# A graph-network kernel: GpSimd waits for every twelfth of its gathers and scatters to land

## The chip, the cores and the metric

The kernel runs on one core of one Trainium2 chip. The metric is the device time of one execution in microseconds (us). The time before is 6714.79 us, the median of 3 runs (6712.42 to 6715.54).

## The reference, cut to what matters

Four blocks of graph layers run one after another over 6250 nodes with 128 features and 106250 edges sorted by target. Each block is added to its input and normalised over the features.

```python
def _sage_conv(h, src, dst, Wl, bl, Wr):          # block 0, twice: stages 0 and 1
    agg = segment_sum(h[src], dst) / maximum(deg, 1.0)[:, None]
    return agg @ Wl.T + bl + h @ Wr.T
def gcn_conv(x, edge_index, W, b):                # block 1 once, block 2 twice: stages 2, 3, 4
    h = x @ W
    return segment_sum(h[src] * (dinv[src] * dinv[dst])[:, None], dst) + b
for l in range(3):                                # block 3: nine "hops", stages 5 to 13
    out = h @ W[l, 0]; x = h
    for k in (1, 2, 3):
        x = segment_sum(w[:, None] * x[src], dst)  # w = dinv[src] * edge_weight * dinv[dst]
        out = out + x @ W[l, k]
    h = relu(layernorm(h + out + bias[l]) * gamma[l] + beta[l])
x = layernorm(x + block(x))
```

So there are 14 sums over neighbours, which the kernel calls stages, and each needs all rows of the one before.

## The kernel before, in words

The nodes make 49 tiles of 128 (`TILES`). In each stage TensorE forms the sum over neighbours in two ways at once, as a `Split` lays down.

**Dense tiles.** For most target tiles the kernel has a matrix in HBM: `counts` (bf16, how many edges join two nodes) for stages 0 to 4, `weights` (float32) for stages 5 to 13. SyncE loads it into `room` in units, and TensorE multiplies every source tile with it (`sweep`, L1130 for bf16 in three parts, L1134 for float32). A stage of 0 to 4 (`EARLY` and its kin) has 41 dense tiles in 11 groups, nine of them four tiles wide. A hop stage (`LATE`) has 31 dense tiles in 8 groups, seven four tiles wide and one three wide; each group takes 49 blocks, one for each source tile.

**Sparse tiles.** The other 8 (in a hop stage 18) target tiles are summed from their edges. GpSimd gathers 128 source rows at a time from `table` in HBM into one of 36 slots of `ring_f` (`fast`, L690: one indirect DMA of 64 KB). A pair of tiles takes 36 gathers, so a stage of 0 to 4 has 144 and a hop stage has 324. VectorE builds a one-hot matrix for each (L1707), and TensorE multiplies them (`edges`, L1164) in batches of three gathers, of which a hop stage has 108. TensorE's program is one fixed order: the sweep is cut into beats of some three blocks, and each batch of `edges` stands behind a beat (`beat_of`). A batch waits for its gathers by `chunk_in[slot]`, and everything behind it on TensorE waits as well.

**What paces GpSimd.** Ahead of a gather it waits for the slot to be free (`batch_done`), and for every second gather for the sweep to have come far enough (`unit_used`, by `pace`). At a stage's start it waits until all rows of the last stage are written (`rows_out`); the stage's other work has begun by then.

**Who writes the matrices.** GpSimd scatters ones and edge weights into zeroed HBM, 128 elements in one indirect DMA (`scatter`, L646). `counts` takes three lists of 215, 285 and 225 scatters, all before GpSimd's first gather. 90 of them come first, then 21 gathers of tables (L662), then the rest. `weights` takes 532, which are issued between the gathers of stages 1 to 4, 161, 80, 150 and 141 of them (`QUOTA`). A scatter already waits for those 4 or 5 places back in its list (6 or 7 for `weights`), by `scattered[q]`, since two writes to one place must not meet.

**The start.** Before stage 0, VectorE prepares the lists and TensorE walks over all edges to sum the degrees (`degree_walk`, L981 and L1528, 49 iterations of 42 matmul records). GpSimd scatters meanwhile. Stage 0's sweep follows the walk; its first sparse batch stands at beat 108 of 182.

Of the kernel before, what the change touches and what calls it, by code (L numbers as in the profile page):

```python
# [139 lines left out]
def landed_by(which, q):  # L140
    return sum(p.lap for p in LISTS[:which] if q < p.laps)
# [4 lines left out]
PAIR0 = [sum(p.pairs for p in SPLITS[:a]) for a in range(STG + 1)]  # L146
# [15 lines left out]
WB = SPAN // HB  # L162
assert SPAN % HB == 0 and HOTS * WIN <= (SPAN - 7) * P and SPAN >= MIX + 3 and SPAN >= BODY
AHEAD_UNITS = 6


def pace(a, c):
# [36 lines left out]
def program(nc, A, out):  # L204
    ctx = ExitStack()
    with ctx:
# [6 lines left out]
        def sem(name):  # L213
            return ctx.enter_context(nc.semaphore(name))
# [174 lines left out]
        scattered = [sem(f"scattered{q}") for q in range(QS)]  # L389
        v_begun, off_ready, fast_rows, p_fast, v_x, in_h, fast_go, parts_rdy = names(  # L390
            "v_begun off_ready fast_rows p_fast v_x in_h fast_go parts_rdy")
        chunk_in = [sem(f"chunk_in{c}") for c in range(CHP)]
# [228 lines left out]
        @block.gpsimd  # L621
        def _(pool):
            pool.iota(iota_i[:, :], pattern=[[1, P]], base=0, channel_multiplier=0).then_inc(g_const, 1)
            pool.iota(ci[:, :], pattern=[[P, CG]], base=0, channel_multiplier=1).then_inc(g_const, 1)
            pool.iota(step_i, pattern=[[1, STEPS]], base=0, channel_multiplier=0).then_inc(g_const, 1)
            pool.memset(ones[:, :], 1.0).then_inc(g_const, 1)
            pool.memset(ident[:, :], 0.0).then_inc(g_const, 1)
            pool.wait_ge(g_const, 5)
            pool.affine_select(out=ident[:, :], in_=ident[:, :], compare_op=ALU.not_equal, fill=1.0, base=0,
                               pattern=[[-1, P]], channel_multiplier=1).then_inc(g_const, 1)  # L630

            for c in range(CHP):
                pool.memset(lows[:, :, c:c + 1], float(LOWS[c])).then_inc(g_lows, 1)

            def scatter(which, i):
                p, m = LISTS[which], (weights if which == NC else counts).rearrange("s (n a) -> (s n) a", a=1)
                r, q = divmod(i, p.laps)

                beside = (q + 1) % p.laps
                if r or which:  # L640
                    if landed_by(which, q) + r:
                        pool.wait_ge(scattered[q], (landed_by(which, q) + r) * 16)
                    if landed_by(which, beside) + r + (q == p.laps - 1):
                        pool.wait_ge(scattered[beside], (landed_by(which, beside) + r + (q == p.laps - 1)) * 16)
                at = q * p.lap + r
                pool.indirect_dma_start(  # L646
                    out=m, out_offset=bass.IndirectOffsetOnAxis(ap=lane_idx[which][:, at:at + 1], axis=0),
                    in_=lane_val[which][:, at:at + 1], in_offset=None).then_inc(scattered[q], 16)

            pool.wait_ge(lanes_ready, 1)  # L650
            wait_zeroed(pool, zeroed_counts, ZQ, 4 * CUTS[1])
            for i in range(AHEAD_OF_ROWS):
                scatter(0, i)

            pool.wait_ge(off_ready, 1)
            pool.wait_ge(e_out, 96)
            blocks = [(k, rows_d.bitcast(I32), e_dst) for k in range(RBLOCKS)]
            blocks += [(k, rows_w, e_wgt) for k in range(RBLOCKS)] + [(k, rows_s.bitcast(I32), e_src) for k in range(WBLOCKS)]
            for k, rows_, pad in blocks:
                n = min(RB * CHP, (PAIRS - 1 - k * RB) * CHP + MIX + 3)  # L660
                runs = pad.rearrange("(e a) -> e a", a=1)
                pool.indirect_dma_start(out=rows_[0:n, k, :], out_offset=None, in_=runs[:, :],  # L662
                                        in_offset=bass.IndirectOffsetOnAxis(ap=off_i[0:n, k:k + 1], axis=0)
                                        ).then_inc(window_rows if pad is e_dst and k < WBLOCKS else fast_rows, 16)

            def fast():
                for i in range(AHEAD_OF_ROWS, LISTS[0].lane):
                    scatter(0, i)
                for which in range(1, NC):
                    pool.wait_ge(lanes_ready, which + 1)  # L670
                    wait_zeroed(pool, zeroed_counts, ZQ, 4 * CUTS[which + 1])
                    for i in range(LISTS[which].lane):
                        scatter(which, i)
                pool.wait_ge(lanes_ready, NC + 1)
                assert sum(QUOTA) == LISTS[NC].lane
                for a, p in enumerate(SPLITS):
                    rows_from = A["x"] if a == 0 else tables[a % 2]
                    if a:
                        pool.wait_ge(rows_out, GROUP0[a] * 16)
                    if a == 1:  # L680
                        wait_zeroed(pool, zeroed_weights, 1, LATE.zeros)
                    put = 0
                    for c in range(p.pairs * CHP):
                        pair, slot = divmod(c, CHP)
                        if PAIR0[a] + pair > 0:
                            freed = (PAIR0[a] + pair - 1) * STP + slot
                            pool.wait_ge(batch_done, freed // HB + 1)
                        if a and c % 2 == 0 and pace(a, c) > 0:
                            pool.wait_ge(unit_used, UNIT0[a] + pace(a, c))
                        pool.indirect_dma_start(out=ring_f[:, slot, :], out_offset=None, in_=rows_from[:, :],  # L690
                                                in_offset=bass.IndirectOffsetOnAxis(ap=f_src[:, c:c + 1], axis=0)
                                                ).then_inc(chunk_in[slot], 16)
                        while 0 < a < STAGES and put * p.pairs * CHP < (c + 1) * (QUOTA[a] - WINDOW):
                            scatter(NC, sum(QUOTA[:a]) + put)
                            put += 1
                    while 0 < a < STAGES and put < QUOTA[a]:
                        scatter(NC, sum(QUOTA[:a]) + put)
                        put += 1

            def whole(way):  # L700
                for q in range(LISTS[0].laps):
                    pool.wait_ge(scattered[q], len(range(q, AHEAD_OF_ROWS, LISTS[0].laps)) * 16)
                pool.wait_ge(pad_out, 48)
                pool.wait_ge(v_walk, 1)
                for k in range(CG):
                    for rows_, pad in ((dstep, dst_pad), (wstep, wgt_pad)):
                        pool.indirect_dma_start(out=rows_[:, k, :], out_offset=None, in_=pad[:, :],
                                                in_offset=bass.IndirectOffsetOnAxis(ap=chunk_idx[:, k:k + 1], axis=0)
                                                ).then_inc(walk_dma, 16)
                stages(pool, way, gather)  # L710

            def gather(way, a, kind, layer):
                if kind == 0:
                    pool.wait_ge(v_tabs, 1)
                    pool.wait_ge(x_copied, 16)
                else:
                    pool.wait_ge(table_done, a * (GROUPS * 16))
                    pool.sem_inc(pool_go, 1)

                def lap(it, n):  # L720
                    for s in range(0, n, SUB):

                        pool.wait_ge(pe_step, way.step(a) + it * RING + (s + SUB - NQ))
                        if s % NQ == 0:
                            pool.wait_ge(idx_staged, a * (way.chunks // NQ) + it * (RING // NQ) + (s // NQ + 1))
                        pool.sem_inc(pool_go, 1)
                        for c in range(s, s + SUB):
                            pool.indirect_dma_start(out=ring[:, c, :], out_offset=None, in_=table[:, :],
                                                    in_offset=bass.IndirectOffsetOnAxis(ap=stage[:, c:c + 1], axis=0)
                                                    ).then_inc(landed[c % NQ], 16)  # L730
                laps, rest = divmod(way.chunks, RING)
                with pool.Fori(0, laps) as it:
                    lap(it, RING)
                if rest:
                    lap(laps, rest)
            ways(pool, "pool", fast, whole)
# [1285 lines left out]
```

## Time and profile before

| | |
|---|---|
| time, median of 3 runs | 6714.79 us |
| span of the profiled execution, first to last instruction | 8546.7 us |
| mean granted TensorE clock in it | 0.929 |
| TensorE busy (PE) | 6464.8 us, 76% |
| GpSimd busy (POOL) | 4719.2 us, 55% |
| VectorE busy (DVE) | 2178.6 us, 25% |

The profiled execution has no time of its own beside its span. Its span is 1831.9 us (27%) longer than the median of the runs, so a duration from the trace has to be weighed before it is set into a run's time. On the page the second part cuts the span into 40 equal slices; each digit is the busy share in tenths, 9 standing for 90% or more.

### The profile page before, as it was taken

Reading aid. Unit: us, or ns where it says so; the run is one execution under the profiler, and the core shown is the slowest. Engines: PE = TensorE matmul, PEld = TensorE weight load, DVE = VectorE, ACT = ScalarE, POOL = GpSimd, SP = SyncE. Lnnn points to the kernel's source line nnn. Section 1 sums busy time; section 2 is a strip of 40 time slices with the busy share of each in tenths; the row PEclk is TensorE's granted clock in tenths of the full one; section 3 lists DMA queues with packets and bytes.
Section 4 is the critical chain, followed back from the end, with each engine's and each line's share of the span. In section 5 each row is a group of like instructions: output and inputs, shape, how many; then the busy total and the mean of one; then the engine's idle time right before and its main releaser. Section 6 shows DMA issues by size and latency. Waiting matters only on the chain.

```text
span 8546.7 us, 79040 instructions
## 1 busy us (share of the span) xinstructions
PE 6464.8 (76%) x27152; PEld 3836.3 (45%) x27153; DVE 2178.6 (25%) x8464; ACT 316.1 (4%) x856; POOL 4719.2 (55%) x4960
## 2 busy tenths in 40 slices
PE   0003039998878787896998988888888898989888
PEld 0003039655544444443554544455444454554444
DVE  8235014222222211121221223222121231212144
ACT  0000000000000000000000000000000000000000
POOL 3766740034545466464656656565565656656565
PEclk9999999999988888997998999999999999999999
DMA  9047000365546554564676767666667676667776
GB/s 369 5 187 299 0 11 0 122 190 153 166 126 205 167 169 146 182 193 170 248 242 233 253 243 251 241 245 232 240 250 241 249 256 230 243 238 253 254 251 220
DMA packets 605834, 1703.64 MB, mean 199 GB/s; under 512 B 132490, under 2 KB 351043, under 8 KB 503944
## 3 DMA queue, kind: packets, MB, share of 16 engines
q1 hardware_dynamic: 340474, 1337.92, 44.4%
q0 software_dynamic: 157616, 240.14, 9.6%
q10 hardware_dynamic: 107388, 120.98, 4.0%
q8 instruction: 205, 3.36, 0.2%
q14 instruction: 151, 1.24, 0.0%
HBM read 1476.47 MB, written 223.40 MB: 199 GB/s over the span
## 4 chain that ended last, share of the span: by engine, by line
PE 64%; another core or an unknown queue 17%; issue 13%; DVE 3%; SPq 1%; ACT 1%; DMA 0%; DVEq 0%; POOL 0%; ACTq 0%; POOLq 0%
PE pwide L1134 32%; PE pwide L1130 15%; PE pstep L1164 8%; PE pstep L981 5%; PE pwide L1222 1%; SPq L537 0%; DVE ring_f L1329 0%; PE pwide L1180 0%; PE pwide L1221 0%; DVE lane_val L1335 0%; DVE lane_val L1336 0%; SPq L517 0%; DVE ring_f L1332 0%; PE pwide L1184 0%
## 5 line engine op out<-in xcount | busy, mean ns | idle before, releaser
L690 POOL DMA_INDIRECT ring_f<-table,f_src x3492 | 3319.3, 951 | 2553.9 <-issue 933.9
L1134 PE MATMUL pwide<-room,acc 128*128 128x512 f32 (+1 forms) x3920 | 1856.4, 612 | 88.6 <-issue 83.3
L1134 PE MATMUL pwide<-room,hcur 128*128 128x512 f32 (+1 forms) x3136 | 1486.8, 611 | 69.5 <-issue 68.1
L1164 PEld LDWEIGHTS pstep<-hot,ring_f 128*128 128x128 f32 x7272 | 1047.7, 199 | 739.0 <-issue 670.2
L1164 PE MATMUL pstep<-hot,ring_f 128*128 128x64 f32 x7272 | 1014.7, 272 | 315.1 <-issue 296.6
L1707 DVE TENSOR_SCALAR hot<-iota,f_win,f_wgt 128x64 f32<-128x64 f32 x2916 | 720.5, 328 | 2053.1 <-PE pstep L1164 856.5
L981 PE MATMUL pstep<-acc,hot 128*128 x2058 | 445.4, 350 | 850.7 <-DVE deg_sums L1533 611.8
L1134 PEld LDWEIGHTS pwide<-room,acc 128*128 128x128 f32 x3920 | 735.0, 199 | 786.1 <-issue 740.0
L1130 PE MATMUL pwide<-room 128*128 128x512 bf16 (+2 forms) x2695 | 1012.7, 377 | 52.0 <-issue 51.2
L646 POOL DMA_INDIRECT counts<-lane_val,lane_idx x725 | 712.7, 983 | 399.5 <-issue 243.8
L1130 PE MATMUL pwide<-room,hcur 128*128 128x512 bf16 (+2 forms) x2695 | 829.6, 374 | 59.2 <-issue 50.4
L1134 PEld LDWEIGHTS pwide<-room,hcur 128*128 128x128 f32 x3136 | 585.5, 198 | 632.7 <-issue 594.0
L981 PEld LDWEIGHTS pstep<-acc,hot 128*128 128x128 f32 x2058 | 444.5, 332 | 851.6 <-issue 851.6
L1130 PE MATMUL pwide<-room,acc 128*128 128x512 bf16 (+2 forms) x2156 | 638.7, 379 | 39.2 <-issue 38.8
L646 POOL DMA_INDIRECT weights<-lane_val,lane_idx x532 | 521.5, 980 | 163.2 <-issue 159.2
L690 POOL DMA_INDIRECT ring_f<-in_x,f_src x144 | 140.6, 976 | 673.0 <-PE pstep L1164 618.5
L1130 PEld LDWEIGHTS pwide<-room 128*128 128x128 bf16 x2695 | 269.6, 100 | 358.6 <-issue 108.1
L1130 PEld LDWEIGHTS pwide<-room,hcur 128*128 128x128 bf16 x2695 | 272.3, 103 | 327.4 <-issue 96.0
L1730 DVE SCALAR_TENSOR_TENSOR xres<-pwide,dinv,xres 128x128 f32<-128x128 f32 x294 | 83.4, 344 | 1015.9 <-remote 546.6
L1130 PEld LDWEIGHTS pwide<-room,acc 128*128 128x128 bf16 x2156 | 217.2, 103 | 257.4 <-issue 81.5
L1730 DVE SCALAR_TENSOR_TENSOR zz<-pwide,dinv,xres 128x128 f32<-128x128 f32 x196 | 55.5, 344 | 741.4 <-remote 421.0
L1528 DVE TENSOR_SCALAR hot<-iota,f_dst 128x128 f32<-128x128 f32 x1029 | 209.6, 285 | 108.0 <-remote 57.9
(318 smaller groups left out, 2486.7 us busy)
## 6 DMA issues: line engine op xcount, KB each, us to landing
room<-weights SPq DMA_DIRECT2D x693, 1024.0 KB
room<-counts SPq DMA_DIRECT2D x495, 512.0 KB
room<-weights SPq DMA_DIRECT2D x162, 768.0 KB
weights<-zz SPq DMA_DIRECT2D x56, 1792.0 KB
counts<-zz ACTq DMA_DIRECT2D x44, 1568.0 KB
ring_f<-table,f_src POOLq DMA_INDIRECT x3492
room<-counts SPq DMA_DIRECT2D x100, 384.0 KB
room<-weights SPq DMA_DIRECT2D x63, 512.0 KB
```

The costliest lines, as they stand in the source:

```text
L646: pool.indirect_dma_start(out=m, out_offset=bass.IndirectOffsetOnAxis(ap=lane_idx[which][:, at:at + 1], axis=0), in_=lane_val[which][:, at ...
L690: pool.indirect_dma_start(out=ring_f[:, slot, :], out_offset=None, in_=rows_from[:, :], in_offset=bass.IndirectOffsetOnAxis(ap=f_src[:, c: ...
L981: ins = pe.matmul(pstep[0][:, 0:2], hot[:, j, :], degree_of[:, bass.ds(it * SPAN + j, 1), :].rearrange("p c a -> p (c a)"), start=j == 0, ...
L1130: ins = pe.matmul(bank[:, 0:w * P], part[:, first + o, :], room_short[:, n % SLOTS, o * w * P:(o + 1) * w * P], start=begins and i == 0, s ...
L1134: ins = pe.matmul(bank[:, 0:w * P], x_of(a)[:, first + o, :], room[:, n % SLOTS, o * w * P:(o + 1) * w * P], start=begins, stop=ends)
L1164: ins = pe.matmul(bank[:, low:low + WIN], row, one, start=begins, stop=ends and not own, skip_group_check=True)
L1222: ins = pe.matmul(o, z, w3[:, of + k, :], start=True, stop=True)
L1528: ins = V.tensor_scalar(hot[:, j, :], iota[:, :], f_dst_flat[:, bass.ds(it * SPAN + j, 1)], None, ALU.is_equal)
L1707: return V.tensor_scalar(to, iota[:, 0:WIN], at, f_wgt[:, pair * CHP + c:pair * CHP + c + 1], ALU.is_equal, ALU.mult)
L1730: ins = V.scalar_tensor_tensor(to[:, j, :], po[:, j, :], scale_of(kind)[:, first + j:first + j + 1], more(j), ALU.mult, ALU.add)
```

## The change

After every twelfth gather of a stage (counted from the stage's start) GpSimd waits until this gather has landed, before it does anything else. After every twelfth scatter of a list (counted from the list's start) it waits until this scatter is written. Nothing else is changed; no instruction moves.

```diff
+REST_AT = 12
@@ scatter(which, i)
                 pool.indirect_dma_start(
                     out=m, out_offset=bass.IndirectOffsetOnAxis(ap=lane_idx[which][:, at:at + 1], axis=0),
                     in_=lane_val[which][:, at:at + 1], in_offset=None).then_inc(scattered[q], 16)
+                if i % REST_AT == REST_AT - 1:
+                    pool.wait_ge(scattered[q], (landed_by(which, q) + r + 1) * 16)
@@ fast(), in the loop over the gathers c of stage a
                         pool.indirect_dma_start(out=ring_f[:, slot, :], out_offset=None, in_=rows_from[:, :],
                                                 in_offset=bass.IndirectOffsetOnAxis(ap=f_src[:, c:c + 1], axis=0)
                                                 ).then_inc(chunk_in[slot], 16)
+                        if c % REST_AT == REST_AT - 1:
+                            pool.wait_ge(chunk_in[slot], (PAIR0[a] + pair + 1) * 16)
                         while 0 < a < STAGES and put * p.pairs * CHP < (c + 1) * (QUOTA[a] - WINDOW):
                             scatter(NC, sum(QUOTA[:a]) + put)
```

## Rows read from the trace of the kernel before

**Rows 1.** The page's first and second part: busy time, and 40 slices.
```profile
PE 6464.8 (76%) x27152; PEld 3836.3 (45%) x27153; DVE 2178.6 (25%) x8464; ACT 316.1 (4%) x856; POOL 4719.2 (55%) x4960
...
PE   0003039998878787896998988888888898989888
...
POOL 3766740034545466464656656565565656656565
```

**Rows 2.** Windows over four hop stages: length, busy of each engine, clock, DMA share, GB/s.
```profile
4480.50:4982.20 501.70, 449.53 (x1582) 250.31 (x1581) 102.17 (x394) 21.49 (x62) 307.73 (x325) 0.92 0.70 248
4982.20:5490.10 507.90, 450.63 (x1549) 251.35 (x1548) 148.39 (x611) 25.83 (x75) 307.00 (x324) 0.92 0.71 249
6008.60:6519.00 510.40, 447.27 (x1582) 250.61 (x1581) 102.59 (x392) 21.49 (x62) 308.72 (x325) 0.92 0.70 244
7023.30:7540.20 516.90, 452.29 (x1702) 262.44 (x1701) 100.70 (x378) 27.50 (x75) 305.96 (x324) 0.92 0.68 235
```

**Rows 3.** Line L690 in 4982.2:5490.1: min/median/max ns; idle until, us, times.
```profile
L690 POOL DMA_INDIRECT ring_f<-table,f_src x324: 938/944/1141, 4982.2 to 5455.6; - x162
...
  issue: 86.4, 278
  PE pstep L1164: 32.1, 23
  DMA table<-acc: 27.6, 1
  PE pwide L1134: 25.6, 16
  remote: 23.3, 6
```

**Rows 4.** Timeline of POOL at a hop stage's start: gathers 1, 2, 3 and 12.
```profile
7023.26 0.94 POOL L690 DMA_INDIRECT ring_f<-table,f_src  x1 [32.99 <-DMA table<-acc]
7024.51 0.94 POOL L690 DMA_INDIRECT ring_f<-table,f_src  x1 [0.30 <-issue]
7025.76 0.94 POOL L690 DMA_INDIRECT ring_f<-table,f_src  x1 [0.30 <-PE pwide L1134]
...
7037.05 0.94 POOL L690 DMA_INDIRECT ring_f<-table,f_src  x1 [0.30 <-issue]
```

**Rows 5.** Timeline of PE there, where it waits for gathers to land.
```profile
7027.67 0.63 PE L1164 MATMUL pstep<-hot,ring_f 128*128 128x64 f32 x4 [1.97 <-DMA ring_f<-table,f_src]
7029.67 0.69 PE L1164 MATMUL pstep<-hot,ring_f 128*128 128x64 f32 x2 [1.37 <-DMA ring_f<-table,f_src]
...
7042.81 0.43 PE L1164 MATMUL pstep<-hot,ring_f 128*128 128x64 f32 x2 [0.91 <-DMA ring_f<-table,f_src]
```

**Rows 6.** Timeline of PE in a stretch of a hop stage without a stall.
```profile
5037.69 2.79 PE L1134 MATMUL pwide<-room,acc 128*128 128x512 f32 x6
5040.32 0.78 PE L1164 MATMUL pstep<-hot,ring_f 128*128 128x64 f32 x6
5040.94 1.94 PE L1134 MATMUL pwide<-room,acc 128*128 128x512 f32 x4
5042.71 1.05 PE L1222 MATMUL pwide<-w,zz 128*128 128x128 f32 x8
5043.60 0.78 PE L1164 MATMUL pstep<-hot,ring_f 128*128 128x64 f32 x6
```

**Rows 7.** The chain of work: the degree walk, and a sweep in bf16.
```profile
738.63 9.13 PE pstep L981 x42
748.31 9.13 PE pstep L981 x42
...
1627.08 30.43 PE pwide L1130 x141
```

**Rows 8.** Windows of the start (columns as in rows 2).
```profile
312.00:470.00 158.00, 0.00 (x0) 0.00 (x0) 39.38 (x108) 0.00 (x0) 120.02 (x124) 1.00 0.02 0
470.00:604.00 134.00, 0.00 (x0) 0.00 (x0) 44.32 (x84) 0.00 (x0) 89.79 (x87) 1.00 0.52 211
...
801.00:1220.00 419.00, 49.13 (x233) 51.74 (x233) 24.61 (x111) 0.00 (x0) 289.28 (x298) 1.00 0.11 38
```

**Rows 9.** Waits of POOL, whole run: in total us, times, longest.
```profile
POOL ring_f L690 <- PE pstep L1164: 960.7, 197, 604.7
```

**Rows 10.** Waits of POOL in stage 1 (2010.7:2566), same columns.
```profile
POOL ring_f L690 <- PE pwide L1130: 90.7, 19, 12.7
POOL ring_f L690 <- DMA table<-zz: 52.5, 1, 52.5
...
POOL weights L646 <- DMA weights<-lane_val,lane_idx: 0.6, 2, 0.3
```

**Rows 11.** Timeline of POOL: the first list's second scatter, and its sixth.
```profile
85.17 0.98 POOL L646 DMA_INDIRECT counts<-lane_val,lane_idx  x1 [0.31 <-issue]
...
92.26 0.97 POOL L646 DMA_INDIRECT counts<-lane_val,lane_idx  x1 [2.30 <-DMA counts<-lane_val,lane_idx]
```

## The prediction

> **What bounds the kernel now.** The page first [rows 1]: from the seventh slice on TensorE (PE) is busy eight or nine tenths, GpSimd (POOL) four to six. That names TensorE. But busy counts only the 0.94 us in which GpSimd works on a gather; what matters is from one start to the next. The windows over hop stages [rows 2] show a period of 502 to 517 us with some 450 us of TensorE and 307 of GpSimd. The waits of line L690 in one of them [rows 3] show the rest: 324 gathers at 944 ns, 86.4 us of "issue" (the 0.30 us between two starts, of which the timeline is full [rows 4]), 27.6 us at the start for the last stage's rows, and 32.1+25.6+23.3 = 81 us for slots and pace, of which some 14 us are again the 0.30 us of those 45 times. So GpSimd needs 324 x 1.25 = 405 us and 28 to 33 us of start: 433 to 438 us in a period of 508. Its true slack in the trace is about 70 us a hop stage, not the half that the digits suggest.
>
> **How the trace stands to the runs.** The span is 1832 us over the median of 6714.79, so the runs have less slack still. I rebuild the run from stretches without a stall. A hop stage on TensorE: three blocks of L1134 take 2.63 us (5037.69 to 5040.32), so 0.877 a block, 7 x 49 blocks make 301 us, and the three wide group's 49 at three quarters 32 us; a batch of L1164 takes 0.62 us (5040.32 to 5040.94), 108 make 67 us; the work behind 13 groups of tiles at 0.9 us for one, two or more such each, 27 us [rows 6]. Sum 427 us. A stage of 0 to 4: 141 records of L1130 in 30.43 us, 0.216 each [rows 7]; 9 x 49 x 3 make 286 us, the two narrow groups 40, the batches 30, the rest 35: about 390. The walk is 49 x 9.69 = 475 us [rows 7]. The start up to its end is 1582 us in the trace, but the stretch 801:1220 holds six iterations (58 us) in 419, and 312:604 holds 84 us of VectorE in 292 [rows 8]; without these stalls, and with 20 us kept for a load that VectorE awaits there, it is about 1030. Total 1030 + 5 x 390 + 9 x 427 + 30 for the end = 6853, 2% over the median. I read that as: in the runs TensorE is at full pace nearly throughout, and a hop stage takes about 420 us.
>
> Then GpSimd must keep up with 420. With 25 us for the stage's start (28 to 33 in the trace, scaled), a gather can take at most 395/324 = 1.22 us from start to start. The ends for this price p are 0.944 (its own duration alone) and 1.25 (as traced, which would make a hop stage 430 and the total too long). I take 1.17, near the traced end, since the duration is steady and only the 0.30 us beside it is what a run without a recorder could shorten. So GpSimd has 404 of 420 us: 16 us of slack.
>
> **What the change adds.** 60 waits in stages 0 to 4 (12 each), 243 in the hops (27 each), and for scatters 17+23+18 = 58 in the lists of counts and 13+7+12+12 = 44 in stages 1 to 4. Nothing is removed or moved. The instruction behind a wait is the next gather or scatter, and everything of GpSimd stands in that line. The price of one wait is the time from the end of GpSimd's instruction to the landing, L. The trace has it where TensorE waits for a gather [rows 4, 5]: the second ended at 7025.45, and its matmuls begin at 7027.67 (2.2 us); the third at 7026.70 and 7029.67 (3.0); the twelfth, the first that would be waited for, at 7037.99 and 7042.81 (4.8). Below, L could be near 2, above near 4.8. I take 2.5, since the first two have TensorE standing ready and the third may have had another cause for part of it.
>
> The Trainium skill, "DMA: Bandwidth & Descriptors", section "Anatomy of one DMA — SWDGE (gpsimd) path", gives a fixed 2.0 us for a DMA issued by GpSimd, most of it the receipt of the last write, plus bytes over 436 GB/s: 2.15 us for 64 KB. The trace's smallest, 2.2, agrees. By that page alone the hop term below would be 27 x 2.15 = 58 us a stage in place of 68.
>
> *Hop stages.* GpSimd before: 324 x 1.17 + 25 = 404, under TensorE's 420. After: 404 + 27 x 2.5 = 472. TensorE is fed in its fixed order and the ring is empty at a stage's start (gather 1 comes only when the sweep is under way, and TensorE already waits for it [rows 5]), so the 36 slots give no cushion against a slower feeder. The period goes from 420 to 472: +52, times 9 = **+468 us**.
>
> *Stages 1 to 4.* Slower start: 52.5 us in the trace [rows 10], 43 taken. Stage 1 has 144+161 = 305 issues: 357 + 43 = 400 (TensorE 390), after it 25 waits of 2 us more, 450: +50. Stage 2: 224 issues, 305 us, after it 343 under 390: 0, hidden by the sweep. Stage 3: 294, 387, then 24 waits: 435, +45. Stage 4: 285, 376, then 424: +34. Together **+129 us**. I take 2 us here since matrices of bf16 load HBM less, and a scatter is smaller. For a scatter's landing the trace has an upper row only: the second ended at 86.15 and the sixth, which waits for it, starts at 92.26 after its usual 0.30, so 5.8 us, while HBM is being zeroed [rows 11]; later the waits 6 or 7 places back cost nothing [rows 10]. The lower bound is 0.
>
> *Start and stage 0.* 58 waits at 0.8 to 2 us delay GpSimd by 45 to 115 us. Cover: it then stands 604.7 us until TensorE's first batch in the trace [rows 9]. In a run the walk ends near 1030 and the first sparse batch comes 108/182 of a stage later, near 1240; GpSimd has its scatters done near 1040 and the first 36 gathers near 1085, so about 150 us cover it. The third list is needed at the eighth group, near 1240 too. Price 0; with the cover gone, up to +100. Stage 0's 108 gathers behind the first ring have 80 beats, 1.5 us each or more: enough.
>
> Sum: 6714.79 + 468 + 129 = 7312, say **7310 us**.
>
> **The rivals.**
> - *Forecast, 0.58:* GpSimd becomes the bound in the hops, by 30 to 65 us a stage: 7080 to 7450.
> - *GpSimd is already at its traced pace in the runs, or L is nearer 3 (0.17).* Then no slack hides anything: 27 x 2.7 = 73 a hop stage, 657, and 50+48+46 early, and 20 of the start: 7535. For it speaks that 0.30 stands unchanged in all rows of POOL; against it the total of 6853, already too long without it.
> - *GpSimd is quicker than 1.1 from start to start (0.19).* With 1.05 it takes 340 + 25, plus 68 is 433 against 420: +13 x 9, early +20, so 6850; with 1.0 nothing shows. In the trace itself the 81 us of waits for slots nearly cover 68 us. For it speaks that slack, against it that a run has 90 us a stage less than the trace, which can only come off this slack.
> - *The wait is met when it is reached (0.02):* a landing within the 0.30 us between starts; no change. [Rows 5] exclude it for gathers.
> - *Other side, faster (0.04):* while GpSimd issues without a pause, TensorE and VectorE stand: 801:1220 loses 361 us [rows 8]. If that is in the runs too, a pause of 1 to 2 us in every 15 gives back a tenth, 35 us at the start, and some 10 us of stall a hop stage; it decides if GpSimd has 70 us of slack in a run as in the trace: 6640. The sum of 6853 speaks against such stalls in the runs. The Trainium skill, "SBUF — State Buffer", section "Who interferes with whom", has an exclusive lock between VectorE and GpSimd that could be such a stall; no row shows it as one.
>
> **How the numbers follow.** A measurement tells 0.2% (13 us) from nothing. Slower by more: 0.58 + 0.17 + 0.14 of the third = 0.89; within: the third's other 0.05 and the 0.02 of a wait that is met = 0.07; faster: 0.04. The range reaches from the quick rival's 6850, leaving out what of it and of the fast one lies below (near 0.14), to the second's 7535 above, leaving out an L of 3 and more: 6850 to 7540.
>
> **What the profile after should show.** 303 waits of L690 for ring_f's own DMA, idle 2.8 us on average with the 0.30; GpSimd's waits for slots and pace in a hop stage down from 81 to under 40 us; TensorE waiting for ring_f in every hop stage, not in a few; hop periods of 510 to 550 in the trace, the span 8700 to 9050, for there the slack is larger than in the runs. The start: stage 0's sweep begins where it did. Wrong would be the price p if the time rises under 200 us with the waits at 2.5 us each; wrong L if the waits are under 1.5 us; wrong the reading of the runs if trace and runs rise alike.

## The result, and the profile after

| | before | after |
|---|---|---|
| time, median of 3 runs | 6714.79 us | 7676.65 us (7647.36 to 7689.74) |
| ratio | | 1.1425 (95%: 1.1391 to 1.1458) |
| span of the profiled execution | 8546.7 us | 7645.5 us |

The change costs 962 us. The forecast was 7310 and its range ended at 7540, so it is 367 us short and outside its range. The span of the trace after is the time of a run; that of before was not. The execution behind [rows 1 to 11] was unlike every other one that was recorded in this study, which matters for all that follows.

The page after, first and second part (answers to [rows 1]):

```profile
span 7645.5 us, 79062 instructions
...
PE 6364.7 (83%) x27152; PEld 3789.7 (50%) x27153; DVE 2182.1 (29%) x8464; ACT 316.6 (4%) x856; POOL 4715.5 (62%) x4960
...
PE   0039996999889989789989888998898899988887
...
POOL 2666766666666666666665665656666656566565
PEclk9755598999999999999999999999999999999999
```

The windows over four hop stages after, with the columns of [rows 2]:

```profile
3632.90:4136.90 504.00, 447.79 (x1582) 249.97 (x1581) 103.78 (x393) 21.54 (x62) 307.46 (x325) 0.96 0.74 247
4136.90:4639.80 502.90, 450.26 (x1549) 248.04 (x1548) 148.42 (x609) 25.85 (x75) 306.72 (x324) 0.95 0.75 252
4639.80:5137.90 498.10, 449.50 (x1707) 258.96 (x1706) 102.37 (x381) 27.55 (x75) 305.90 (x324) 0.96 0.73 244
5137.90:5640.30 502.40, 444.69 (x1582) 247.79 (x1581) 103.98 (x393) 21.54 (x62) 308.34 (x325) 0.96 0.74 248
```

A period of 502 us looks like that of [rows 2]. The periods of before that it has to be held against are about 428 us; they come below, from a second profile of the kernel before.

The gather's line in the third of these windows (answers to [rows 3]): idle until, us, times, and from issue to landing.

```profile
  issue: 104.0, 264
  DMA ring_f<-table,f_src: 81.7, 24
  PE pwide L1139: 7.3, 14
  PE pstep L1169: 6.7, 22
...
DMA to landing us min/median/max: 2.5/3.8/6.2
```

24 of the 27 waits bear the name of the gather's own landing, 81.7/24 = 3.40 us each with the usual 0.30. The waits for slots and pace are down to 14 us, 36 times, of which 11 us are again the 0.30: TensorE hardly ever holds GpSimd up. The timeline of GpSimd around two of the waits:

```profile
4707.06 0.94 POOL L693 DMA_INDIRECT ring_f<-table,f_src  x1 [0.30 <-issue]
4708.31 0.99 POOL L693 DMA_INDIRECT ring_f<-table,f_src  x1 [0.30 <-issue]
4712.61 0.94 POOL L693 DMA_INDIRECT ring_f<-table,f_src  x1 [3.32 <-DMA ring_f<-table,f_src]
...
4726.34 0.94 POOL L693 DMA_INDIRECT ring_f<-table,f_src  x1 [0.30 <-issue]
4730.70 0.94 POOL L693 DMA_INDIRECT ring_f<-table,f_src  x1 [3.42 <-DMA ring_f<-table,f_src]
```

One gather, 1.25 us from start to start, and once in twelve 4.3 us. TensorE in the same 33 us:

```profile
4702.47 0.69 PE L1169 MATMUL pstep<-hot,ring_f 128*128 128x64 f32 x2 [3.66 <-DMA ring_f<-table,f_src]
...
4719.12 0.43 PE L1169 MATMUL pstep<-hot,ring_f 128*128 128x64 f32 x2 [0.21 <-DMA ring_f<-table,f_src]
...
4723.02 0.43 PE L1169 MATMUL pstep<-hot,ring_f 128*128 128x64 f32 x2 [0.44 <-DMA ring_f<-table,f_src]
```

It stands three times for a gather that has only now landed: it takes each one as it comes. Over the whole run it waits like this for 608 us (first row; the second is stage 0, where it stands 61.3 us for the first gather), and GpSimd's waits for landings are these:

```profile
PE pstep L1169 <- DMA ring_f<-table,f_src: 608.1, 450, 15.8
...
PE pstep L1169 <- DMA ring_f<-in_x,f_src: 75.5, 20, 61.3
```

```profile
POOL ring_f L693 <- DMA ring_f<-table,f_src: 762.5, 234, 6.0
POOL counts L647 <- DMA counts<-lane_val,lane_idx: 233.5, 141, 6.6
...
POOL ring_f L693 <- DMA weights<-lane_val,lane_idx: 81.1, 29, 3.9
...
POOL weights L647 <- DMA ring_f<-table,f_src: 67.1, 23, 4.5
```

### The profile page after: what moved, and what is told of

Its sections match the earlier page's. It is cut to its first block and busy times, and to the rows that moved or that the text cites. A ratio compares the mean times of both kernels' runs of the same rounds, so it can differ in the third digit from the quotient of the medians.

```text
span 7645.5 us, 79062 instructions
## 1 busy us (share of the span) xinstructions
PE 6364.7 (83%) x27152; PEld 3789.7 (50%) x27153; DVE 2182.1 (29%) x8464; ACT 316.6 (4%) x856; POOL 4715.5 (62%) x4960
## 5 line engine op out<-in xcount | busy, mean ns | idle before, releaser
L1139 PE MATMUL pwide<-room,acc 128*128 128x512 f32 (+1 forms) x3920 | 1827.3, 608 | 37.3 <-DMA room<-weights 37.3
L1169 PE MATMUL pstep<-hot,ring_f 128*128 128x64 f32 x7272 | 1073.2, 274 | 688.8 <-DMA ring_f<-table,f_src 608.1
L1139 PE MATMUL pwide<-room,hcur 128*128 128x512 f32 (+1 forms) x3136 | 1470.7, 611 | 0.0
L647 POOL DMA_INDIRECT counts<-lane_val,lane_idx x725 | 716.6, 988 | 501.5 <-DMA counts<-lane_val,lane_idx 233.5
L1135 PE MATMUL pwide<-room 128*128 128x512 bf16 (+2 forms) x2695 | 995.8, 370 | 0.0
L1135 PE MATMUL pwide<-room,acc 128*128 128x512 bf16 (+2 forms) x2156 | 615.6, 370 | 0.5 <-ACT zz L788 0.5
L788 ACT ACTIVATE zz<-pwide 128x512 f32<-128x512 f32 (+2 forms) x127 | 73.3, 577 | 4350.3 <-PE pwide L1139 2855.5
L1711 DVE TENSOR_SCALAR hot<-iota,f_win 128x64 f32<-128x64 f32 x720 | 131.7, 272 | 278.6 <-PE pstep L1169 276.4
```

The lines of the kernel that those rows point to most:

```text
L647: pool.indirect_dma_start(out=m, out_offset=bass.IndirectOffsetOnAxis(ap=lane_idx[which][:, at:at + 1], axis=0), in_=lane_val[which][:, at ...
L788: act.activation(zT, bank[:, 0:w * P], ACT.Copy).then_inc(z_done, 1)
L1135: ins = pe.matmul(bank[:, 0:w * P], part[:, first + o, :], room_short[:, n % SLOTS, o * w * P:(o + 1) * w * P], start=begins and i == 0, s ...
L1139: ins = pe.matmul(bank[:, 0:w * P], x_of(a)[:, first + o, :], room[:, n % SLOTS, o * w * P:(o + 1) * w * P], start=begins, stop=ends)
L1169: ins = pe.matmul(bank[:, low:low + WIN], row, one, start=begins, stop=ends and not own, skip_group_check=True)
L1711: return V.tensor_scalar(to, iota[:, 0:WIN], at, None, ALU.is_equal)
```

## The experiments

The theories: **A**, GpSimd issues at 1.25 us in the runs as in the trace and bounds the whole run, so each pause is paid, wherever it stands; **B**, the forecast's account (slack of 16 us in a hop stage, stage 2 and the start covered).

**1. The waits of the lists of counts alone (58), ahead of stage 0.**

```diff
-                if i % REST_AT == REST_AT - 1:
+                if which < NC and i % REST_AT == REST_AT - 1:
```

The gathers' waits are taken out.

> Only the 58 waits in the three lists of counts (17+23+18), none on gathers or weights. Theory A (GpSimd is the bound of the whole run, from its first scatter on, at 1.25 us from start to start as traced): each wait is paid in full, 58 x 1.8 = +105 us on 6715. Theory B (the forecast: GpSimd has some 150 us of cover at the start, TensorE bounds there): no change, 0 to +15 us.

Measured: 6799.06 us, ratio 1.0116 (1.0099 to 1.0133), +80. B's cover of 150 us isn't there, only a small one: in this run's trace stage 0's first gather starts at 1253.07, 107 us later than in the second profile of before (1145.71, experiment 8), and of these GpSimd gets 22 us back in its wait ahead of stage 1, which is 22.6 us in place of 44.4.

**2. The waits of the hop stages alone (243).**

```diff
-                        if c % REST_AT == REST_AT - 1:
+                        if a >= STAGES and c % REST_AT == REST_AT - 1:
```

The scatters' waits are taken out.

> Only the 243 waits on gathers of the nine hop stages. Theory A: 243 x 2.35 = +571 us, since GpSimd has no slack. Theory B, with 16 us of slack a stage and L 2.5: +468 us; with L 2.35: +427 us.

Measured: 7383.7 us, 1.0995 (1.0976 to 1.1015), +664: 73.8 a stage, 2.73 for each wait. That is over both expectations, and nearest to the rival's 657.

**3. The waits of stages 0 to 4 alone (60 of gathers, 44 of scatters).**

```diff
-                if i % REST_AT == REST_AT - 1:
+                if which == NC and i % REST_AT == REST_AT - 1:
@@
-                        if c % REST_AT == REST_AT - 1:
+                        if a < STAGES and c % REST_AT == REST_AT - 1:
```

> Only the 60 waits on gathers of stages 0 to 4 and the 44 on scatters of weights. Theory A: 104 x 2.1 = +218 us, stage 0 and stage 2 included, and with e1 and e2 it adds up to the 962 us of the whole change. Theory B: +129 us, nothing from stages 0 and 2.

Measured: 6919.56 us, 1.0298 (1.0281 to 1.0315), +200. The three parts make 944 of the 962 us: the cost lies in all of them and adds up.

**4. Half as many waits.**

```diff
-REST_AT = 12
+REST_AT = 24
```

> All waits, but every twenty-fourth instead of every twelfth: some 200 waits. Theory A (no slack, each wait paid): half of 962, +480 us. Theory B (the slack is used up first): a hop stage 404 + 14 x 2.4 = 438 against 420, +18 x 9, and +60 early: +220 us. In the profile: if the trace of before is long because GpSimd never pauses, this one's span should lie between, above its own run's time.

Measured: 7199.54 us, 1.0712 (1.0694 to 1.073), +480, half of 962 (481). With slack, the first waits would have been free and half of them would have cost less than half. The span was 7204.5 us, the time of its runs. This also ended an idea that I held for a while, that the long trace of before came from a GpSimd that never pauses.

**5. All 303 waits of gathers, each on the gather six places back.**

```diff
-                            pool.wait_ge(chunk_in[slot], (PAIR0[a] + pair + 1) * 16)
+                            pool.wait_ge(chunk_in[slot - 6], (PAIR0[a] + pair + 1) * 16)
```

The scatters' waits are taken out.

> Every twelfth gather's place waits for the gather six places back, which by the trace landed within 4.8 us and was issued 6 x 1.25 us earlier: a wait instruction that is met when it is reached; no waits on scatters. If the price of the change is the time to the landing: no change on 6715. If a wait as such breaks up GpSimd's stream (a restart cost of its own), +303 times that cost, 30 us for 0.1.

Measured: 6718.04 us, 1.0006 (0.9996 to 1.0015). Over the 303 waits the interval runs from −3 to +10 us, so a wait instruction that is met when it is reached costs 0.03 us at most; what costs is the landing.

**6. The kernel before with less work for TensorE.**

```diff
+                elif o == 1 and not begins and not ends and o != nb - 1:
+                    return
```

> The kernel before, in which TensorE leaves out the second block of each unit of weights that is at least three tiles deep in the hop stages: 12 of 49 blocks in each group, about 82 us of TensorE a stage; loads, waits and GpSimd's work are unchanged. The output is not the reference's. Theory A (GpSimd is the bound): 6715 less at most some 5 us a stage at the hand-over, so 0 to -50 us. Theory B (420 of TensorE over 404 of GpSimd): -16 a stage, -144 us. TensorE alone as the bound: -700 us.

Measured: 6674.28 us, 0.9943 (0.9927 to 0.996), −38 us. The blocks left out are some 80 us a hop stage at the pace of [rows 6]; TensorE's busy time falls by less, by about 50 us: each of the remaining records of the sweep takes longer (615 ns in the mean in place of 589), at a mean granted clock of 0.95 where it was 0.99 to 1.00. One hop stage of this trace (columns of [rows 2]), which in the second profile of before takes 429.70 us with 424.55 of TensorE:

```profile
4118.10:4539.80 421.70, 375.03 (x1518) 224.23 (x1517) 103.32 (x382) 27.54 (x75) 306.57 (x324) 0.95 0.83 289
```

TensorE then waits for ring_f instead. Its waits in that trace, and in the next experiment's:

```profile
PE pstep L1166 <- DMA ring_f<-table,f_src: 476.2, 482, 5.9
```

```profile
PE pstep L1166 <- DMA ring_f<-table,f_src: 25.7, 18, 5.8
```

**7. The kernel before with every twelfth gather of the hops not issued (243 of 2916).**

```diff
+                        if a < STAGES or c % 12 != 11:
+                            (the indirect DMA of fast(), as before)
@@
+                if a < STAGES or i % 12 != 11:
+                    (the wait of TensorE for it, as before)
```

> The kernel before, in which every twelfth gather of the hop stages is not issued and TensorE does not wait for it (it multiplies what the slot held): 27 of 324 gathers a stage, 34 us of GpSimd. The output is not the reference's. Theory A: -34 x 9 = -304 us, or less where TensorE becomes the bound at its own 400 to 420 us a stage. Theory B: 0, TensorE bounds already.

Measured: 6651.09 us, 0.9909 (0.9892 to 0.9925), −62 us: 7 of the 34 us a stage that GpSimd has less. Now GpSimd waits for TensorE. Its waits from 4300 to 6600 us in this trace come to 0.60 us each in the first row, where the 331 of the whole second profile of before (experiment 8) are 0.33 us each; and a hop stage in which TensorE never stands:

```profile
POOL ring_f L691 <- PE pstep L1166: 114.8, 192, 6.2
POOL ring_f L691 <- PE pwide L1135: 60.6, 111, 4.9
```

```profile
4554.71:4970.06 415.35, 415.35 (x1582) 237.30 (x1581) 105.04 (x392) 21.49 (x62) 282.52 (x297) 1.00 0.87 295
```

Experiments 6 and 7 together place the bound: taking work from TensorE gives 4 us a stage, from GpSimd 7, and then the other one holds. Against a period of about 428 us, GpSimd alone would need about 424 and TensorE alone about 421. So the two are close in the kernel before, but whatever is added to GpSimd's line makes it the later one nearly at once.

**8. The kernel before, unchanged, profiled again.**

> The kernel before once more, for a second trace of it. Its time: 6715 us, no change. Open is the span: if the recorder itself stretches a kernel whose GpSimd never pauses, about 8500 us again; if the first trace caught one odd execution, 6720 us, with the stalls of TensorE and VectorE in the start gone, hop stages of about 430 us, and GpSimd in them with no idle time beside the 0.30 us between gathers.

Measured: 6721.51 us, 1.0002 (0.9993 to 1.0012), and its span is the time of a run. First the page, and the windows over four hop stages and the start:

```profile
span 6713.0 us, 79040 instructions
...
PE 6076.4 (91%) x27152; PEld 3685.3 (55%) x27153; DVE 2184.9 (33%) x8464; ACT 316.2 (5%) x856; POOL 4725.7 (70%) x4960
```

```profile
3715.70:4146.40 430.70, 422.46 (x1554) 237.83 (x1553) 149.35 (x611) 25.84 (x75) 306.65 (x324) 1.00 0.86 296
4146.40:4576.10 429.70, 424.55 (x1702) 250.12 (x1701) 101.35 (x378) 27.49 (x75) 306.01 (x324) 0.99 0.83 282
4576.10:4999.00 422.90, 417.61 (x1582) 238.17 (x1581) 104.66 (x393) 21.48 (x62) 308.14 (x324) 1.00 0.87 294
...
801.00:1220.00 419.00, 401.97 (x1959) 276.39 (x1960) 112.16 (x476) 8.64 (x15) 311.63 (x323) 1.00 0.45 131
```

The gather's line in the second of these windows, and GpSimd's timeline at two places: the hand-over from the lists of counts to stage 0, and from stage 2 to stage 3.

```profile
L690 POOL DMA_INDIRECT ring_f<-table,f_src x324: 940/944/1016, 4146.4 to 4549.9; - x162
...
  issue: 83.8, 275
  DMA table<-hcur: 25.6, 1
  PE pstep L1164: 10.1, 33
  PE pwide L1134: 4.6, 15
```

```profile
1144.35 1.05 POOL L646 DMA_INDIRECT counts<-lane_val,lane_idx  x1 [0.31 <-issue]
1145.71 1.17 POOL L690 DMA_INDIRECT ring_f<-in_x,f_src  x1 [0.30 <-issue]
...
2081.31 0.96 POOL L646 DMA_INDIRECT weights<-lane_val,lane_idx  x1 [0.31 <-issue]
2082.57 0.97 POOL L690 DMA_INDIRECT ring_f<-table,f_src  x1 [0.30 <-issue]
```

This is the profile that the prediction should have had. The 81 us of waits for slots and pace [rows 3] are 14.7 us, 48 times the 0.30. All 324 gathers stand 1.25 us apart, 404 us from the first start to the last, and the rest of the period is the hand-over of the rows. TensorE is 98 to 99% busy in a hop stage and GpSimd 71 to 73%, and yet GpSimd is the later of the two. The two hand-overs show it in the early part: the last scatter of counts is followed by stage 0's first gather after 0.30 us, and stage 2's last scatter likewise by stage 3's first gather. The window 801:1220 has TensorE busy for 402 us where [rows 8] have 49.

**9. The 243 waits of the hops, on the gather before the last.**

```diff
-                            pool.wait_ge(chunk_in[slot], (PAIR0[a] + pair + 1) * 16)
+                            pool.wait_ge(chunk_in[slot - 1], (PAIR0[a] + pair + 1) * 16)
```

Otherwise as experiment 2.

> As e2 (243 waits in the hop stages), but each waits for the gather before the last instead of the last, which was issued 1.25 us earlier. If a wait costs the time to a landing: 2.73 - 1.25 = 1.5 us each, +360 us in place of the 664 of e2. If it costs a fixed sum for emptying or restarting GpSimd's DMA queue: +664 us again.

Measured: 7132.15 us, 1.0612 (1.0594 to 1.063), +413, 1.70 us for each. A landing of 3.0 us less one spacing of 1.25 leaves 1.75; a fixed price of a wait that blocks would have stayed at 2.73. Held against experiment 2, the wait has become 1.03 us cheaper, a little less than one spacing.

**10. The same 243 places, but GpSimd works for 2 us there in place of waiting.**

```diff
-                            pool.wait_ge(chunk_in[slot], (PAIR0[a] + pair + 1) * 16)
+                            for n in range(2):
+                                rests[0] += 1
+                                pool.memset(f_dst_flat, 0.0).then_inc(g_const, 1)
+                                pool.wait_ge(g_const, 6 + rests[0])
```

> As e2, but in place of the landing GpSimd writes zeros twice to a table of 128 x 1029 that is no longer read, some 2.2 to 2.6 us in each of the 243 places. Theory A (any time of GpSimd is paid in full): 243 x 2.4 = +580 us. If it is the empty DMA queue that costs, and not GpSimd's time: nothing near that, below +200 us. Theory B of the forecast, 16 us of slack a stage: +440 us.

Measured: 7145.47 us, 1.063 (1.0612 to 1.0648), +426, 1.75 us for each. The memsets were shorter than I had assumed. GpSimd's timeline:

```profile
5006.33 0.95 POOL L694 DMA_INDIRECT ring_f<-table,f_src  x1 [0.31 <-issue]
5007.28 1.99 POOL L700 MEMSET f_dst<- 128x1029 f32 x2
5009.53 0.95 POOL L694 DMA_INDIRECT ring_f<-table,f_src  x1 [0.27 <-POOL f_dst L700]
```

From the end of a gather to the next one's start it is 2.25 us, 1.95 more than the usual 0.30. Of the 243 pauses 8 fall into a hand-over between two hop stages, in which GpSimd waits anyway (a stage's last gather is its 324th, a twelfth one), and one stands behind the very last gather. The other 234 make 456 us. The eight hand-overs, from the end of a stage's last gather to the start of the next one's first, are shorter than in the second profile of before, 156 us together against 187. 456 − 31 = 425, and 426 was measured. The same sum for experiment 2, with hand-overs of 158 us: (664 + 29)/234 = 2.96 us for a landing. So each microsecond of pause inside a stage is paid, less some 4 us a stage that the hand-over gives back, and what counts is GpSimd's time, not the drained queue of its transfers.

**11. The waits of stage 2 alone (19).**

```diff
-                if i % REST_AT == REST_AT - 1:
+                if which == NC and sum(QUOTA[:2]) <= i < sum(QUOTA[:3]) and i % REST_AT == REST_AT - 1:
@@
-                        if c % REST_AT == REST_AT - 1:
+                        if a == 2 and c % REST_AT == REST_AT - 1:
```

> Only stage 2's waits: 12 on its gathers and 7 on its scatters. Theory A (GpSimd bounds in stage 2 too, whose sweep has two bf16 parts instead of three): 19 x 1.9 = +36 us. The forecast's step (stage 2 has 390 us of TensorE over 305 of GpSimd, so its waits are hidden): 0.

Measured: 6749.57 us, 1.0051 (1.0037 to 1.0064), +35. The stage for which the forecast had 0, "hidden by the sweep", pays like the others: 1.86 us for each wait, against 1.93 for the 104 of experiment 3.

**12. A version that might be faster: the hops' sparse batches are spread over one beat less, so that the last one stands a beat earlier.**

```diff
-LATE = Split([4, 4, 4, 4, 2], [4] * 7 + [3], 9, -2, last=2)
+LATE = Split([4, 4, 4, 4, 2], [4] * 7 + [3], 9, -1, last=2)
```

> A try at a faster kernel: the kernel before with the hop stages' sparse batches spread over one beat less (the last one stands one beat, 3.2 us of TensorE, earlier), no waits added. If the hand-over after the last gather has TensorE's beat on its path: up to -3 us a stage, -25 us. If the last gather's landing, 3 us, is the later of the two: 0. If batches that come earlier only wait more: 0 to +10 us.

Measured: 6730.8 us, 1.0026 (1.0016 to 1.0037), +17. No version that does all the work is faster than the kernel before (those of experiments 6 and 7 leave some out).

## Why the prediction was wrong, point by point

**Right: what the change does.** The instruction behind a wait is the next gather, all of GpSimd's line stands behind it, the ring gives no cushion, and GpSimd sets the time. The 303 waits came as written, and so did TensorE waiting for ring_f in every hop (48.4 us in the window above, 5.1 in one of the second profile of before). The waits for slots and pace stand at 14 us, as forecast under 40, but that is no merit: they were 14.7 before the change. The hop periods, forecast at 510 to 550, are 498 to 504 in the four windows above. TensorE's 427 us of a hop stage, rebuilt from rows without a stall, is near: experiment 7 puts its floor at about 421.

**Wrong: the price p = 1.17, and with it 16 us of slack.** It is 1.25 us in every trace, 404 us for 324 gathers, and the hand-over takes the rest of the 428. In a hop stage there is no slack but some 4 us in the hand-over; +52 was to be +74. Of these 22 us, 16 are the slack; the rest is the next point, less what falls into the hand-over. Over nine stages it is 664 in place of 468, 196 us.

**Why p went wrong: the sum of 6853.** It was 2% over the median and I used it to rule out p = 1.25. The misfit lay elsewhere. The records of the sweep (L1130) in stages 2 and 3 of the second profile of before, and in stage 2 of the first one: length, PE busy (records), clock, DMA share, GB/s.

```profile
1756.50:2065.30 308.80, 236.95 (x1078) 0.97 0.80 251
2065.40:2443.40 378.00, 336.92 (x1617) 1.00 0.73 211
```

```profile
2544.90:2964.90 420.00, 252.75 (x1078) 0.86 0.58 185
```

A stage of 0 to 4 has 539 blocks (11 groups of 49). Stage 2 has two records for each, as `parts_of` in the kernel says, and the sum had three: it put down 390 us for a sweep that takes 309. The first trace had this count too. And stage 0's sweep starts at 967 us, not at 1030. These two make 144 of the 157 us by which the five sweeps end before the sum's 1030 + 5 x 390 = 2980 (at 2823). The nine hops and the end fit the sum to 17 us, and for them p = 1.25 would have fitted as well. A sum made of one engine's work, with a bound that was assumed to be TensorE in all stages, can't tell a price of another engine to 6%. I took a misfit of 138 us, which came from a start and five stages that I had not rebuilt group by group, for evidence on the nine hops.

**Wrong: L = 2.5 us.** 234 waits of the trace after make 762.5 us, 3.26 each, 2.96 without the usual 0.30, and 3.10 in the window above. The 2.2 us was a misreading of [rows 5]: the row at 7027.67 holds four records, two for each gather, so it starts with the first gather, which had ended at 7024.20. That is 3.5 us for the first, not 2.2 for the second; with 3.0 for the third and 4.8 for the twelfth nothing in these rows spoke for 2.5. The Trainium skill, "DMA: Bandwidth & Descriptors", section "Anatomy of one DMA — SWDGE (gpsimd) path", makes it 2.15 us for 64 KB, and the agreement that I saw with it rested on the same misreading; the measured mean of 3.0 decides, in windows in which 244 to 252 GB/s are moved. The Trainium skill, "DMA: Bandwidth & Descriptors", section "Latency and other measured facts", says that HBM's access latency is the main part of the fixed cost and is higher under load; whether that is the difference no run here shows.

**Wrong: start and stage 0 at nothing.** The cover of 150 us supposed that GpSimd has its scatters done near 1040 and that TensorE comes to its first sparse batch near 1240. In the second profile of before the scatters are done at 1145, the first gather follows after 0.30 us, and TensorE is there at 1176.81:

```profile
1176.81 0.78 PE L1164 MATMUL pstep<-hot,ring_f 128*128 128x64 f32 x6
```

The 604.7 us of waiting in [rows 9] belong to that one execution, in which the walk stalled. The landing waits of the counts' scatters rose from 124.4 us in the second profile of before to 233.5 us, and stage 0's first gather moved from 1145.71 to 1250.56. Of these 105 us the shorter wait ahead of stage 1 (44.4 us before, 18.2 after) takes 26; experiment 1 paid +80. "Stage 0's sweep begins where it did" is nearly so (967 and 982 us), but that was the wrong thing to look at: its gathers began 105 us later.

**Wrong: stage 2 at 0, and 129 us for stages 1 to 4.** Experiment 11 paid +35 in stage 2 alone, experiment 3 +200 for the 104 waits of stages 0 to 4. The cover of stage 2 was the third record of each block, which there isn't: the forecast's own 343 us for GpSimd after the change lie 34 us above the sweep's 309. The two engines are close there as well: in stage 2 of the second profile of before TensorE is busy for 292 of 304.5 us, and GpSimd waits for the sweep for 24.3 us, 20 times, so a part of the 19 waits is covered. In the other stages p and L were too low, as in the hops, and stage 0 had been put at nothing.

The parts: hops +196, stages 0 to 4 +71, start +80 over the forecast, together 347 of the 365 us between the sum of 7312 and the median; 18 are what the parts measured apart lack to the whole.

**The rival that was right** is the second, "GpSimd is already at its traced pace in the runs, or L is nearer 3": its 657 us for the hops stand against 664 measured. I gave it 0.17, and its 7535 has 144 us for stages 1 to 4 and 20 for the start, where 200 and 80 were paid. "For it speaks that 0.30 stands unchanged in all rows of POOL": that was the direct evidence, against it stood only a sum. **The test that I had named** ("wrong the reading of the runs if trace and runs rise alike") came out in a way that I had not thought of: the trace after is 901 us shorter than that of before, while the runs rose by 962. The sign named for a wrong p (under 200 us) didn't show either, since p was wrong to the other side. The forecast of 8700 to 9050 for the span rested on the belief that a recorder makes the trace long. It doesn't; that one execution was odd.

**The hand-overs.** That they are some 4 us shorter each with the change has to do with TensorE. The eight of them come to 187 us in the second profile of before, to 149 us in experiment 6, where TensorE has less work and GpSimd is no slower (these 38 us are about all that it gained), and to 277 us in experiment 7, where TensorE is the later one (10 of them for the stage's last gather, which isn't issued there). So before the change the end of TensorE's work for a stage still stands in them, and with the pauses it does less.

**Open.** What stalled TensorE and VectorE in the first trace of before; it was seen in none of the 13 later ones.

## What to carry to other kernels

Count an engine that issues DMAs from start to start, not by its busy digits: here 0.94 us of work and a 0.30 us gap made an engine at 70% the bound over one at 91%, and every microsecond added inside a stage was paid, but for some 4 us a stage. Where the span of a profiled execution is far from the runs' time, its waits and covers (slack, "hidden behind", engines that stand) aren't those of a run; only the durations and spacings of undisturbed stretches may be used, and a rebuilt sum that fits to 2% (and here had the records of one stage wrong) must not overrule a spacing that stands unchanged in all rows. On the engine that ends last, a wait for the landing of the transfer just issued costs the whole landing (3.0 us here), a wait on the one before it 1.0 us less, and one six places back nothing.

## What the runs showed of the hardware that was not expected

- An execution of this kernel can be recorded at 8546.7 us where another one is at 6713.0 and the medians of the runs lie between 6712.78 and 6721.51: in the stretch 801:1220 TensorE did 49 us of work in the one and 402 us in the other, while GpSimd kept at 289 and 312.
- GpSimd's spacing of two gathers, where it waits for nothing, is 1.25 us in the odd execution, in the good one, and after the change.
- The granted clock was 0.99 to 1.00 on average in the hop windows of before and 0.95 to 0.96 in those after, where TensorE stands for some 50 us of 500: the higher of its two levels (2.4 GHz) for some nine tenths of the time, the lower one (1.2 GHz) for the rest. Its busy time for the same stages goes from some 421 to 448 us. In the stage of experiment 6 that is shown above TensorE stands for 47 us as well, with GpSimd unchanged, and the clock is again 0.95.
